# Stage one of a token mixer: rows turned by transposing DMAs instead of TensorE, and a second residual buffer

## The chip, the cores and the metric

The kernel runs on one core of a Trainium2 chip. The metric is the device time of one execution in microseconds (us), the median of several runs. TensorE is called PE in the profile (PEld is its weight load), VectorE DVE, ScalarE ACT, GpSimd POOL, SyncE SP; an engine's name with a q behind it is its sequencer, where DMAs are issued.

## What is computed

The input is a set of 16 images of 256 by 64 complex coefficients. Four steps follow, the last two over 16 x 257 rows of 512 numbers:

```python
h = _L0_tok_ref(x, L0_tok_log_dt, L0_tok_B_ri, L0_tok_inv_A_real, L0_tok_A_imag, 512)
h = jnp.concatenate([jnp.broadcast_to(cls_tok, (h.shape[0], 1, h.shape[2])), h], axis=1)
h = h + _L0_attn_ref(_layernorm(h, axis=-1), L0_attn_gamma, ..., L0_attn_b_skip)
h = h + _L0_ffn_ref(_layernorm(h, axis=-1), L0_ffn_gate_w, ..., L0_ffn_sw_down)
```

`_L0_tok_ref` makes 256 tokens per image out of powers of complex numbers. `_L0_attn_ref` is a gated recurrence along the tokens (`h = (1 - a) * h + a * b`, times a tanh), with an output projection and a skip projection of the normalized row. `_L0_ffn_ref` is a mixture of eight experts of which each row uses two, plus one shared expert that all rows use: `silu(x @ sw_gate) * (x @ sw_up) @ sw_down`.

## The kernel before

Every number that enters a product is split into two fp16 halves, high and low, and a product is three matmuls (high x high, high x low, low x high); `split3` writes them.

There are two stages. **Stage one** walks through the tokens in blocks of 16 tokens of all 16 images, that is 256 rows or two tiles of 128; block 0 is the class token and has one tile. Per block it makes the tokens, runs the recurrence and the shared expert, stores the sum in `out`, chooses two experts per row, and scatters the normalized rows to `x_slots`, sorted by expert. **Stage two** takes 71 tiles of such rows through their experts and adds the results to `out`. The change lies wholly in stage one.

Each engine has its own instruction list, written by hand, and semaphores are all that ties the lists together. A list is a row of bodies, `body(-1)` to `body(17)`; bodies 3 to 13 are a loop of the hardware, the others are written out. A body works on four blocks at once. `body(k)` does, on PE and in this order:

- gate and up products of the shared expert for block k-1 (line 1025 on; six groups m = 0 to 5, PSUM banks 1, 2, 0 in turn), and after group 3 five small products that rank the rows;
- `project(0)` for block k, tile 0: skip and output projection into banks 4 and 5;
- `shared_down(0)` and `shared_down(1)` for block k-1, both into bank 3 (`BD`);
- `project(1)` for block k;
- the turning of the normalized rows of block k+1: 16 transposes through PE (`transposes`, line 982, `x2w` in the trace), which ACT copies to SBUF as `x2T` (line 1238);
- `features` for block k+2: 64 small fp32 products that make the tokens;
- the turning of the second normalized rows of block k, tile 0 (`rows3`, 8 transposes of `x3w`), which ACT copies as `x3T` (line 1244);
- the input products of block k+1 (`win`, 36 matmuls of 256 columns);
- `rows3` for tile 1, and then the router's products of block k (24 matmuls of 8 columns, `gw`), which wait for ACT's copies.

DVE's list for body k: `gprod` and `glow` multiply gate by up and split the result; `choose` and `place` work on the ranks; `stats2` takes mean and variance of block k+1; `tok_p` and `tok_e` are large elementwise products that feed `features` (`tok_p(n, 5)` is what `features(n)` waits for); line 1554 writes the low half of `x2r`. For each tile it then adds the down product to the residual and writes it to `r_o` (line 1560), adds the projections to the residual `h2` (lines 1569, 1570), takes its mean and variance (1572 to 1577), and, when POOL has made the inverse root (lines 927, 928) and ACT the normalized row and its high half (`rows_hi`, lines 1173, 1177), writes the low half (`rows_lo`, line 1450). The recurrence (`scan`) ends the body.

The second `shared_down` waits until DVE has read bank 3 (`c_dev`), because there is one bank; and line 1569 for block k waits until `r_o` has been made from `h2` of block k-1, because there is one `h2`.

SP issues the plain DMAs: the tokens of a block (`hx`), an expert's weights in and their halves out, the rows of `out`. In `body(16)` it also issues eight rounds of two DMAs that write zero rows behind each expert's rows in `x_slots` (lines 824 to 829); each round first loads two addresses from SBUF into registers. Stage two starts when SP has loaded the first tiles (line 799), which wait for DVE's table (`d_tb`).

## Time and profile before

| | |
|---|---|
| median of 3 runs | 1255.03 us (1254.31 to 1255.35) |
| the profiled execution, its own time | 1255.78 us |
| its span in the trace | 1254.1 us |
| PE busy | 1095.0 us, 87% of the span |
| DVE busy | 817.1 us, 65% |
| stage one, first `features` to first expert product | about 75 to 825 us |
| one body of stage one (bodies 4 to 13) | 42.1 us |

The trace is of one execution. A row of a timeline gives start, length, engine, line of the kernel, instruction, and in square brackets how long the engine had been idle before it and what it waited for. Matmuls are pipelined, so two rows of PE overlap a little, and the distance of two starts is the better measure. The granted clock of PE is 1.00 of its full speed from 300 to 700 us; it lies lower in the first 150 us and again between 790 and 800 us.

### The profile page before, as it was taken

What the parts mean: (1) busy time and instruction counts of PE and PEld (TensorE: products, weight loads), DVE (VectorE), ACT (ScalarE), POOL (GpSimd) and SP (SyncE); (2) the same over time, 40 slices, a digit from 0 to 9 for tenths busy, and PEclk for the clock granted to TensorE, in tenths of its full rate; (3) what the DMA queues carried; (4) which work ended last, traced back from release to release, by engine and by line L of the source; (5) the groups of instructions that cost most, each with busy time, mean ns of one, the idle gap of its engine ahead of it and who ended that gap; (6) DMA issues with size and microseconds to landing.
All of it is one profiled execution on the core that took longest, in us unless ns stands there. A gap on an engine that the chain in (4) does not pass through costs nothing.

```text
span 1254.1 us, 27654 instructions
## 1 busy us (share of the span) xinstructions
PE 1095.0 (87%) x8397; PEld 729.3 (58%) x8398; DVE 817.1 (65%) x2123; ACT 408.2 (33%) x724; POOL 412.3 (33%) x352
## 2 busy tenths in 40 slices
PE   3037889999999999999999999759999999999995
PEld 3035566667666766676667656525555555555552
DVE  7955887888788878887888655433444444444442
ACT  4313444435443544355345542301111111111110
POOL 1001221332233123212321221114555555655554
PEclk8556999999999999999999999899999999999998
DMA  7310243233323332333233329847998787878785
GB/s 250 99 32 22 70 139 107 84 130 129 121 76 138 128 111 87 138 120 109 97 138 121 105 104 374 289 113 181 220 222 135 125 134 130 132 126 137 128 129 71
DMA packets 241446, 166.16 MB, mean 132 GB/s; under 512 B 191522, under 2 KB 210338, under 8 KB 239348
## 3 DMA queue, kind: packets, MB, share of 16 engines
q1 hardware_dynamic: 224852, 120.14, 36.3%
q0 software_dynamic: 15504, 36.46, 14.3%
q10 hardware_dynamic: 1040, 8.91, 1.8%
q8 instruction: 28, 0.46, 0.1%
q14 instruction: 22, 0.18, 0.0%
HBM read 53.40 MB, written 79.73 MB: 106 GB/s over the span
## 4 chain that ended last, share of the span: by engine, by line
PE 64%; DVE 11%; ACT 7%; issue 4%; POOL 4%; DMA 2%; SPq 2%; POOLq 0%; DVEq 0%; ACTq 0%
PE bank L974 24%; PE bank L1136 11%; PE bank L1126 10%; PE bank L1127 10%; PE bank L1058 4%; ACT wexp L1244 2%; POOL inv L927 2%; PE bank L996 2%; DVE r_o L1560 2%; DVE h L1569 2%; ACT wexp L1173 2%; DVE h L1570 1%; DVE stat L1572 1%; POOL off L928 1%; DVE wexp L1328 1%
## 5 line engine op out<-in xcount | busy, mean ns | idle before, releaser
L974 PE MATMUL bank<-wexp 128*128 128x256 f16 (+2 forms) x3252 | 410.7, 288 | 12.4 <-DVE yT L1513 4.1
L974 PEld LDWEIGHTS bank<-wexp 128*128 128x128 f16 x3252 | 312.1, 100 | 92.2 <-issue 11.6
L1126 PE MATMUL bank<-wexp,rows_in 128*128 x852 | 256.8, 314 | 9.5 <-DMA rows_in<-x_slots 3.4
L1127 PE MATMUL bank<-wexp,rows_in 128*128 x852 | 256.2, 314 | 0.0
L952 POOL DMA_INDIRECT out<-x2w,rows_in x71 | 113.6, 1600 | 124.8 <-DMA out<-x2w,rows_in 74.8
L940 POOL TENSOR_TENSOR ex<-base,ld 128x8 f32<-128x8 f32 x71 | 120.1, 1691 | 75.4 <-DVE ld L1617 74.7
L1638 DVE SCALAR_TENSOR_TENSOR mixed<-bank,mixed 128x352 f32<-128x352 f32 x71 | 37.3, 525 | 164.0 <-ACT mixed L1285 123.2
L1285 ACT ACTIVATE mixed<-bank 128x352 f32<-128x352 f32 x71 | 32.9, 464 | 302.5 <-PE bank L1127 294.1
L1058 PE MATMUL bank<-wexp 128*128 128x512 f16 x495 | 114.1, 383 | 17.0 <-DVE r_o L1560 17.0
L904 POOL TENSOR_TENSOR inv<-var,power 128x4 f32<-128x4 f32 x17 | 19.1, 1122 | 316.5 <-DVE var L1506 316.5
L1126 PEld LDWEIGHTS bank<-wexp,rows_in 128*128 128x128 f16 x852 | 83.4, 98 | 68.3 <-issue 27.7
L918 POOL DMA_INDIRECT x_slots<-x3w,sl x66 | 91.9, 1392 | 69.5 <-DVE sl L1395 40.0
L1136 PE MATMUL bank<-wexp,gates 128*128 (+1 forms) x477 | 111.7, 379 | 2.6 <-DVE x2w L1633 2.6
L996 PE MATMUL bank<-wexp 64*128 64x64 f32 x1024 | 67.2, 292 | 49.8 <-DVE wexp L1333 49.8
L1127 PEld LDWEIGHTS bank<-wexp,rows_in 128*128 128x128 f16 x852 | 83.5, 98 | 44.3 <-issue 0.3
L927 POOL TENSOR_TENSOR inv<-var,power 128x1 f32<-128x1 f32 x33 | 35.5, 1076 | 183.5 <-DVE var L1577 183.5
L996 PEld LDWEIGHTS bank<-wexp 64*128 64x128 f32 x1024 | 65.0, 205 | 51.9 <-issue 47.1
L1188 ACT ACTIVATE sgs<-bank 128x256 f32<-128x256 f32 (+1 forms) x102 | 38.4, 376 | 164.2 <-PE bank L974 164.2
L1058 PEld LDWEIGHTS bank<-wexp 128*128 128x128 f16 x495 | 46.1, 98 | 77.3 <-DVE r_o L1560 21.7
L1173 ACT ACTIVATE wexp<-h,off,inv 128x512 f32<-128x512 f32 x33 | 26.8, 813 | 168.4 <-POOL off L928 168.4
L1328 DVE TENSOR_TENSOR wexp<-wexp 128x1024 f32 (+1 forms) x64 | 77.8, 1222 | 0.9
L1136 PEld LDWEIGHTS bank<-wexp,gates 128*128 128x128 f16 (+1 forms) x477 | 46.6, 98 | 52.5 <-issue 3.5
(287 smaller groups left out, 1426.2 us busy)
## 6 DMA issues: line engine op xcount, KB each, us to landing
w_halves<-rows_in SPq DMA_DIRECT2D x16, 704.0 KB
wexp<-w_halves ACTq DMA_DIRECT2D x1, 8704.0 KB
wexp<-w_halves SPq DMA_DIRECT2D x8, 1088.0 KB
h_tok<-tokens SPq DMA_DIRECT2D x16, 512.0 KB, 2.7
mixed<-h_tok SPq DMA_DIRECT2D x32, 256.0 KB
out<-r_o SPq DMA_DIRECT2D x32, 256.0 KB
w_halves<-rows_in SPq DMA_DIRECT2D x16, 384.0 KB
x_slots<-zrow SPq DMA_DIRECT2D x8, 768.0 KB, 5.0
```

Of the source, the lines that this page charges most:

```text
L918: nc.gpsimd.indirect_dma_start(out=xs_d.bitcast(I32), out_offset=bass.IndirectOffsetOnAxis(ap=sl[:, i, c:c + 1], axis=0), in_=x3w[:, i, :] ...
L927: link(TT(inv3[:, i:i + 1], var3[:, i:i + 1], power[:, 0, 0:1], ALU.pow))
L940: nc.gpsimd.tensor_tensor(ex[:, b % 2, 0, :], base[:], ld[:, b % 2, :], ALU.pow).then_inc(d_ex, 1)
L952: nc.gpsimd.indirect_dma_start(out=out_rows, out_offset=bass.IndirectOffsetOnAxis(ap=ext[b][:, E:E + 1].bitcast(I32), axis=0), in_=yo[b % ...
L974: last = MM(dst, stat_of(step, a), mov_of(step, b), start=(s_ == 0 and a + b == 0), stop=(s_ == len(steps) - 1 and a == 1))
L996: last = MM(BU[t][:, j * NA:(j + 1) * NA], pp[q, f, j].rearrange("p b c -> p (b c)"), ea[q, f, j, :], start=(f == 0), stop=(f == 1))
L1058: MM(BD[:], gT[:, m, a, t], wsd[:, m, b, :], start=(m == 0 and a + b == 0), stop=False)
L1126: MM(GB[:, 0:H], xT[b][:, a, c, :], wexp[:, u, o:o + H], start=s_, stop=e_)
L1127: last = MM(UB[:, 0:H], xT[b][:, a, c, :], wexp[:, u, o + H:o + 2 * H], start=s_, stop=e_)
L1136: last = MM(DB[:], gT2[b % 4][0:HK[c], a, c, :], wexp[0:HK[c], bass.ds(unit, 2), o:o + D // 2], start=(c == 0 and a + w == 0), stop=(c == ...
L1173: A(xf[:, i, :], h2[:, i, :], ACT.Identity, bias=off3[:, i:i + 1], scale=inv3[:, i:i + 1]).then_inc(c_xf3, 2 // nt)
L1328: ch.do(TT((pp, pt)[f % 2][:, f // 2], cc, hh, ALU.mult))
```

## The change

Four things are changed.

1. PE turns no rows in stage one. SP issues transposing DMAs from `x2r` to `x2T` and from `x3w` to `x3T` (one per tile, four per body), after the other DMAs of its body and before the stores to `out`. Those of `x2T` for block k+1 wait for `project(1)` of block k. PE and ACT lose the transposes and the copies.
2. `h2` has two buffers, used by turns, and `r_o` is gone: the down product is added in place (`down_out`) and `out` is stored from `h2`. The down products have two banks, 3 and 0.
3. The order on PE becomes gate and up, `project(0)`, `shared_down(0)`, `project(1)`, `shared_down(1)`, `features`, `win`, router.
4. On ACT and DVE the work is in another order: block k+1 is normalized in the middle of block k-1's gate and up work, DVE's line for the low half of `x2r` stands there too, `project_out(1)` stands ahead of the last two `tok_p`, and the token copies (`tok_out`) come later on ACT. The loop of the hardware holds two bodies and runs five times (bodies 4 to 13).

The instructions' order, first PE, from the second projection of a body that is written out to its end (body 2 of before, body 3 of the change; both have the same rows there as the bodies of the loop). The names are the program's: `wexp` is the large buffer in which all weights and turned rows of stage one lie, 128x64 x32 are the products of `features`, 128x256 x36 those of `win`. Before:

```order
L1045 MATMUL bank<-wexp,yT 128x512
L1046 MATMUL bank<-wexp,yT 128x512
L1047 MATMUL bank<-wexp,yT 128x512
L1048 MATMUL bank<-brow,ones_row 128x512
L982 MATMUL bank<-ident,x2w 128x128 x16
L996 MATMUL bank<-wexp 128x64 x32
L982 MATMUL bank<-ident,x3w 128x128 x8
L974 MATMUL bank<-wexp 128x256 x36
L982 MATMUL bank<-ident,x3w 128x128 x8
L974 MATMUL bank<-gw,wexp 128x8 x24
```

Of the change, the rows of the same stretch (here with `shared_down(1)`, which follows the second projection):

```order
L1056 MATMUL bank<-wexp,yT 128x512
L1057 MATMUL bank<-wexp,yT 128x512
L1058 MATMUL bank<-wexp,yT 128x512
L1059 MATMUL bank<-brow,ones_row 128x512
L1069 MATMUL bank<-wexp 128x512 x15
L1072 MATMUL bank<-wexp 128x512
L1073 MATMUL bank<-wexp 128x512
L1008 MATMUL bank<-wexp 128x64 x32
L994 MATMUL bank<-wexp 128x256 x36
L994 MATMUL bank<-gw,wexp 128x8 x24
```

The three rows of transposes (`ident`) are gone, and the second down product stands between the second projection and `features`.

Next SP at the end of `body(16)`: the eighth round of zero rows and what follows it. Before:

```order
L826 ISA
L826 REGISTER_ALU
L826 DMA x_slots<-pads 384x16
L828 ISA
L828 DMA x_slots<-zrow 128x3x512
L846 DMA out<-r_o 8x16x512 [waits c_dev]
L846 DMA out<-r_o 8x16x512
L794 DMA w_halves<-rows_in 128x2816 [waits c_wl]
L795 DMA w_halves<-rows_in 128x1536
```

Of the change:

```order
L826 ISA
L826 REGISTER_ALU
L826 DMA x_slots<-pads 384x16
L828 ISA
L828 DMA x_slots<-zrow 128x3x512
L856 DMA_TRANSPOSE wexp<-x3w 128x8x128 [waits c_up,c_rt,c_lo3]
L856 DMA_TRANSPOSE wexp<-x3w 128x8x128 [waits c_lo3]
L866 DMA out<-h 8x16x512 [waits c_dev]
L866 DMA out<-h 8x16x512
```

The two transposing DMAs of `x3w` for block 16 stand behind the last of the eight rounds, where before PE turned these rows.

Last DVE, from the variance of tile 0 on, in the same two bodies. Before (L1577 is that variance and, further down, that of tile 1; L1333 are `tok_p` 4 and 5, L1450 is `rows_lo(0)`, L1560 `r_o`, L1308 `tok_e`):

```order
L1577 TENSOR_SCALAR var<-mv 128x1
L1333 TENSOR_TENSOR wexp<-wexp 128x1024 x2
L1450 SCALAR_TENSOR_TENSOR x3w<-wexp,x3w 128x512
L1560 SCALAR_TENSOR_TENSOR r_o<-bank,h 128x512
L1569 SCALAR_TENSOR_TENSOR h<-bank,ir,mixed 128x512
L1570 SCALAR_TENSOR_TENSOR h<-bank,h 128x512
L1572 BN_STATS stat<-h 128x6
L1574 BN_AGGR mv<-stat 128x2
L1576 TENSOR_SCALAR neg<-mv 128x1
L1577 TENSOR_SCALAR var<-mv 128x1
L1308 TENSOR_TENSOR wexp<-wexp 128x512 x4
```

Of the change (L1514 is the variance, L1326 `tok_p(3)`, L1519 `down_out(0)`, L1443 `rows_lo(0)` and at the end `rows_lo(1)`, L1506 to L1514 `project_out(1)`, L1331 `tok_p` 4 and 5):

```order
L1514 TENSOR_SCALAR var<-mv 128x1
L1326 TENSOR_TENSOR wexp<-wexp 128x1024
L1519 SCALAR_TENSOR_TENSOR h<-bank,h 128x512
L1443 SCALAR_TENSOR_TENSOR x3w<-wexp,x3w 128x512
L1506 SCALAR_TENSOR_TENSOR h<-bank,ir,mixed 128x512
L1507 SCALAR_TENSOR_TENSOR h<-bank,h 128x512
L1509 BN_STATS stat<-h 128x6
L1511 BN_AGGR mv<-stat 128x2
L1513 TENSOR_SCALAR neg<-mv 128x1
L1514 TENSOR_SCALAR var<-mv 128x1
L1331 TENSOR_TENSOR wexp<-wexp 128x1024 x2
L1443 SCALAR_TENSOR_TENSOR x3w<-wexp,x3w 128x512
```

`tok_p` 4 and 5, for which `features` waits, have moved from ahead of `rows_lo(0)` to behind it and behind the whole of `project_out(1)`.

The diff, cut to its core:

```diff
--- before.py
+++ after.py
...
-        LOOP0, LOOP1 = 3, NCH - 2
+        LOOP0, TRIPS = 4, (NCH - 6) // 2
...
+            with eng.Fori(0, TRIPS) as kk:
                 if chain is not None:
-                    chain.enter(k, LOOP0, per)
-                body(k)
+                    chain.enter(kk, 0, per)
...
+                    if has(k + 1):
+                        n = k + 1
+                        sp.wait_ge(c_lo2, n + 1)
+                        apart(sp, c_sps)
+                        at_least(sp, c_out, n * 2)
+                        apart(sp, c_sps)
+                        for i in range(tiles(n)):
+                            sp.dma_start_transpose(x2T[:, i].rearrange("p h k t -> p (h k) t"),
+                                                   x2r[:, i].rearrange("p h d -> p (h d)")).then_inc(c_e2[i], 16)
+                    if has(k):
+                        n = k
+                        at_least(sp, c_up, n * 6)
+                        apart(sp, c_sps)
+                        at_least(sp, c_rt, n)
+                        apart(sp, c_sps)
+                        for i in range(tiles(n)):
+                            sp.wait_ge(c_lo3, n * 2 + (i + 1) * 2 // tiles(n))
+                            apart(sp, c_sps)
+                            sp.dma_start_transpose(x3T[:, i].rearrange("p h k t -> p (h k) t"),
+                                                   x3w[:, i, 0:2 * D]).then_inc(c_e3[i], 16)
...
-                                sp.dma_start(dst, r_o[:, i, :]).then_inc(c_ro, 16)
+                                sp.dma_start(dst, h2[:, 1 - q, i, :]).then_inc(c_ro, 16)
...
-                def rows3(n, i):
-                    done = n * 2 + (2 if tiles(n) == 1 else i + 1)
-                    pe.wait_ge(c_hi3, done)
-                    pe.wait_ge(c_lo3, done)
-                    if i == 1 and has(n - 1):
-                        pe.wait_ge(c_dev, n * 2)
-                    if has(n + 1):
-                        pe.wait_ge(c_e2, (n + 2) * 2)
-                    transposes(BX[i], x3r[:, i]).then_inc(c_t3, 2 // tiles(n))
...
+                        if m == 2:
+                            at_least(pe, c_dev, n * 2)
...
+                    if has(k - 1):
+                        for m in range(SHM + 1):
+                            gate_up_shared(m)
+                            if m == 3:
+                                ranks()
                     if has(k):
                         project(0)
                     if has(k - 1):
                         shared_down(0)
+                    if has(k) and tiles(k) == 2:
+                        project(1)
                     if has(k - 1) and tiles(k - 1) == 2:
                         shared_down(1)
-                    if has(k) and tiles(k) == 2:
-                        project(1)
-                    if has(k + 1):
-                        n = k + 1
-                        pe.wait_ge(c_hi2, n + 1)
-                        pe.wait_ge(c_lo2, n + 1)
-                        at_least(pe, c_e3, n * 2 - 2)
-                        at_least(pe, c_th, n)
-                        for q in range(tiles(n)):
-                            if q == 1 and has(k - 1):
-                                pe.wait_ge(c_sl, k)
-                            transposes((psum[0], BG)[q], x2r[:, q]).then_inc(c_t2, 2 // tiles(n))
...
+                    if has(k + 1):
+                        n, w, nt = k + 1, cols(k + 1), tiles(k + 1)
+                        for i in range(nt):
+                            pe.wait_ge(c_e2[i], turned_rows(n, i))
+                        at_least(pe, c_th, n)
+                        if has(k - 1):
+                            pe.wait_ge(c_sl, k)
+                        for m in range(3):
                             dst = (BG[:, 0:w], BB[:, 0:w], BG[:, TOK:TOK + w])[m]
-                            last = split3(dst, lambda s_, a: win[:, s_, a, m * S:(m + 1) * S],
-                                          lambda s_, b: x2T[:, b, s_, 0:w], range(KD))
-                            if m == 2:
-                                last.then_inc(c_gt, 1)
-                    if has(k) and tiles(k) == 2:
-                        rows3(k, 1)
+                            last = split3(dst.rearrange("p (i t) -> p i t", t=P), lambda s_, a: win[:, s_, a, m * S:(m + 1) * S],
+                                          lambda s_, b: x2T[:, 0:nt, b, s_, :], range(KD))
+                        last.then_inc(c_gt, 1)
                     if has(k):
                         n = k
                         for i in range(tiles(n)):
-                            pe.wait_ge(c_e3, n * 2 + (i + 1) * 2 // tiles(n))
-                            t = slice(i * P, (i + 1) * P)
-                            last = split3(BS[:, i * E:(i + 1) * E], lambda s_, a: x3T[:, a, s_, t],
+                            pe.wait_ge(c_e3[i], turned_rows(n, i))
+                            if tiles(n) == 1:
+                                pe.wait_ge(c_oev, 2)
+                            elif i == 0:
+                                pe.wait_ge(c_oev, n * 2 + 2)
...
+                def normalized(n):
+                    nt = tiles(n)
+                    act.wait_ge(c_pw2, n + 1)
+                    at_least(act, c_lo3, n * 2 - 2)
+                    for i in range(nt):
+                        last = A(xf[:, i, :], hx[:, i, :], ACT.Identity, bias=off2[:, i:i + 1], scale=inv2[:, 0, i:i + 1])
+                    last.then_inc(c_xf2, 1)
+                    act.wait_ge(c_xf2, n + 1)
+                    for i in range(2):
+                        at_least(act, c_e2[i], turned_rows(n - 1, i))
+                    A(x2r[:, 0:nt, 0, :], xf[:, 0:nt, :], ACT.Copy, scale=SX).then_inc(c_hi2, 1)
...
+                        ghigh(n, 2)
+                    if has(k + 1):
+                        normalized(k + 1)
...
+                    if has(k + 1):
+                        n, nt = k + 1, tiles(k + 1)
+                        at_least(act, c_oev, n * 2)
+                        A(hc[:, 0:nt, :], hx[:, 0:nt, :], ACT.Copy).then_inc(c_prom, 1)
...
+                    def down_out(i):
+                        n, nt = k - 1, tiles(k - 1)
+                        v.wait_ge(c_dn, n * 2 + (i + 1) * 2 // nt)
+                        STT(h2[:, 1 - q, i, :], BD[i][:], 1.0 / SW, h2[:, 1 - q, i, :], ALU.mult, ALU.add).then_inc(c_dev, 2 // nt)
...
-                    if has(k - 1):
+                        glow(k - 1, 0)
+                        gprod(k - 1, 2)
+                    elif tokens2:
+                        for f in range(2):
+                            tok_p(k + 2, f)
+                    if isinstance(k, int) and k == -1:
+                        for f in range(5):
+                            tok_e(1, f)
+                    if has(k + 1):
+                        stats2(k + 1)
...
+                    if shared and tokens2:
+                        tok_p(k + 2, 0)
+                    if shared:
+                        glow(k - 1, 1)
+                        gprod(k - 1, 3)
+                        place(k - 1)
+                        if tokens2:
+                            tok_p(k + 2, 1)
+                    if shared:
+                        glow(k - 1, 2)
+                        gprod(k - 1, 4)
+                    if has(k + 1):
+                        n, nt = k + 1, tiles(k + 1)
+                        v.wait_ge(c_hi2, n + 1)
+                        STT(x2r[:, 0:nt, 1, :], xf[:, 0:nt, :], SX, x2r[:, 0:nt, 0, :], ALU.mult, ALU.subtract).then_inc(c_lo2, 1)
...
+                    if tokens2:
+                        tok_p(k + 2, 2)
+                    if has(k):
+                        project_out(0)
+                    if tokens2:
+                        tok_p(k + 2, 3)
+                    if shared:
+                        down_out(0)
+                    if has(k):
+                        rows_lo(k, 0)
+                    if has(k) and tiles(k) == 2:
+                        project_out(1)
+                    if isinstance(k, int) and k == LAST:
+                        table(1)
+                    if tokens2:
+                        tok_p(k + 2, 4)
+                        tok_p(k + 2, 5)
+                    if has(k) and tiles(k) == 2:
+                        rows_lo(k, 1)
+                    if shared and tiles(k - 1) == 2:
+                        down_out(1)
                     if htok(k + 3):
-                        tok_e(k + 3, 4)
+                        for f in range(4):
...
```

## Rows read from the trace of the kernel before

**Rows 1.** The page, part 1: engine, busy time, share, instructions.

```profile
PE 1095.0 (87%) x8397; PEld 729.3 (58%) x8398; DVE 817.1 (65%) x2123; ACT 408.2 (33%) x724; POOL 412.3 (33%) x352
```

**Rows 2.** Timeline of PE, body 6: start, length (us), engine, line, instruction.

```profile
336.91 10.65 PE L974 MATMUL bank<-wexp 128*128 128x256 f16 x96 [0.26 <-issue]
...
359.93 3.41 PE L1058 MATMUL bank<-wexp 128*128 128x512 f16 x15 [0.88 <-DVE r_o L1560]
...
367.48 1.07 PE L982 MATMUL bank<-ident,x2w 128*128 128x128 f16 x16
368.47 3.79 PE L996 MATMUL bank<-wexp 64*128 64x64 f32 x64
...
372.65 4.09 PE L974 MATMUL bank<-wexp 128*128 128x256 f16 x36
...
378.31 0.46 PE L974 MATMUL bank<-gw,wexp 128*128 128x8 f16 x12 [0.83 <-ACT wexp L1244]
379.03 1.16 PE L974 MATMUL bank<-wexp 128*128 128x256 f16 x9 [0.27 <-issue]
```

**Rows 3.** Timeline of DVE, the same body.

```profile
342.78 0.42 DVE L1356 SCALAR_TENSOR_TENSOR gf<-bank,sgs 128x256 f32<-128x256 f32 x1 [1.28 <-ACT sgs L1188]
...
359.19 0.69 DVE L1560 SCALAR_TENSOR_TENSOR r_o<-bank,h 128x512 f32<-128x512 f32 x1 [1.12 <-PE bank L1062]
360.02 0.75 DVE L1569 SCALAR_TENSOR_TENSOR h<-bank,ir,mixed 128x512 f32<-128x512 f32 x1
...
362.72 2.35 DVE L1333 TENSOR_TENSOR wexp<-wexp 128x1024 f32<-128x1024 f32 x2
366.81 0.69 DVE L1450 SCALAR_TENSOR_TENSOR x3w<-wexp,x3w 128x512 f16<-128x512 f32 x1 [1.75 <-ACT x3w L1177]
```

**Rows 4.** Timeline of POOL, the same body.

```profile
349.16 1.03 POOL L904 TENSOR_TENSOR inv<-var,power 128x4 f32<-128x4 f32 x1 [18.25 <-DVE var L1506]
...
362.99 1.38 POOL L927 TENSOR_TENSOR inv<-var,power 128x1 f32<-128x1 f32 x1 [4.09 <-DVE var L1577]
```

**Rows 5.** Timeline of ACT, body 6.

```profile
353.97 1.52 ACT L1226 ACTIVATE wexp<-mixed,off,inv 128x512 f32<-128x512 f32 x2
355.52 1.06 ACT L1230 ACTIVATE x2w<-wexp 128x1024 f16<-128x1024 f32 x1
```

**Rows 6.** Timeline of PE, bodies -1 to 1.

```profile
83.80 1.01 PE L982 MATMUL bank<-ident,x2w 128*128 128x128 f16 x8 [3.46 <-DVE x2w L1554]
...
110.11 7.09 PE L996 MATMUL bank<-wexp 64*128 64x64 f32 x64 [3.12 <-DVE wexp L1333]
...
123.86 4.18 PE L974 MATMUL bank<-wexp 128*128 128x128 f16 x72
...
161.24 3.98 PE L974 MATMUL bank<-wexp 128*128 128x256 f16 x35
```

**Rows 7.** Timeline of PE, the last bodies of stage one.

```profile
725.60 0.17 PE L1032 MATMUL bank<-m,tri 128*128 128x8 f16 x1
...
765.28 0.17 PE L1032 MATMUL bank<-m,tri 128*128 128x8 f16 x1
...
794.90 13.42 PE L974 MATMUL bank<-wexp 128*128 128x256 f16 x96
...
825.17 0.47 PE L1126 MATMUL bank<-wexp,rows_in 128*128 x1 [3.39 <-DMA rows_in<-x_slots]
```

**Rows 8.** Timeline of DVE, body 16.

```profile
772.63 0.27 DVE L1546 CAST runi<-run 128x8 int32<-128x8 f32 x1
```

**Rows 9.** Timeline of SP's issues, body 16.

```profile
774.69 0.72 SPq L826 DMA_DIRECT2D x_slots<-pads  x1
...
805.37 1.98 SPq L846 DMA_DIRECT2D out<-r_o  x2
```

**Rows 10.** Landing times of line 799's transposing DMAs, stage two.

```profile
L799 SPq DMA_TRANSPOSE rows_in<-x_slots x71: 1246/1253/1777, 821.1 to 1215.1; - x71
...
DMA to landing us min/median/max: 3.0/3.1/6.5
```

More of the change, by code:

```diff
@@ L170, in vit_tower @@
         late = Region(high.ap[:, high.at:])
-        x2T = high.take([P, 2, KD, TOK], F16)
-        x3T = high.take([P, 2, KD, TOK], F16)
+        x2T = high.take([P, 2, 2, KD, P], F16)
+        x3T = high.take([P, 2, 2, KD, P], F16)
         gT = high.take([P, SHM + 1, 2, TOK], F16)
@@ L707, in iterate @@
         def iterate(eng, body, chain=None, per=None):
-            body(-1)
+            body(-1, 1)
             for k in range(LOOP0):
-                body(k)
-            with eng.Fori(LOOP0, LOOP1) as k:
+                body(k, k % 2)
+            with eng.Fori(0, TRIPS) as kk:
                 if chain is not None:
-                    chain.enter(k, LOOP0, per)
-                body(k)
+                    chain.enter(kk, 0, per)
+                for r in range(2):
+                    body(kk * 2 + LOOP0 + r, (LOOP0 + r) % 2)
             if chain is not None:
-                chain.leave(LOOP1 - LOOP0)
-            for k in range(LOOP1, LAST + 1):
-                body(k)
+                chain.leave(TRIPS)
+            for k in range(LOOP0 + 2 * TRIPS, LAST + 1):
+                body(k, k % 2)
+        turned_rows = lambda n, i: n * 16 + (16 if i == 0 else 0)
         has = lambda k: not isinstance(k, int) or 0 <= k <= NCH
@@ L976, in split3 @@
                     return last
-                def transposes(bank, rows):
-                    for h in range(2):
-                        for c in range(KD):
-                            last = nc.tensor.transpose(bank[:].bitcast(F16)[:, (h * KD + c) * P:(h * KD + c + 1) * P],
-                                                       rows[:, h, c * P:(c + 1) * P], ident16[:])
-                    return last
                 def features(k):
@@ L1039, in project @@
                         if i == 0:
+                            for j in range(tiles(n)):
+                                pe.wait_ge(c_e2[j], turned_rows(n, j))
                             pe.wait_ge(c_yh, n + 1)
@@ L1231, in body @@
-                    if has(k):
-                        rows_hi(k, 0)
-                    if has(k + 1):
-                        n, nt = k + 1, tiles(k + 1)
-                        at_least(act, c_out, (k + 1) * 2)
-                        for i in range(nt):
-                            act.wait_ge(c_t2, n * 2 + (i + 1) * 2 // nt)
-                            A(x2T[:, :, :, i * P:(i + 1) * P].rearrange("p h k t -> p (h k) t"),
-                              (psum[0], BG)[i][:].bitcast(F16).rearrange("p (c t) -> p c t", t=P), ACT.Copy).then_inc(c_e2, 2 // nt)
@@ L1240, in rows_t @@
[L1240 to L1245 removed]
+                        n = k - 1
+                        silu(n, 1)
+                        ghigh(n, 0)
+                        silu(n, 2)
@@ L1338, in tok_p @@
                             ch.do(ins)
-                def tokens_p(k, f):
-                    if not isinstance(k, int) or k >= 0:
-                        tok_p(k + 2, f)
                 def glow(n, m):
@@ L1536, in body @@
-                    if has(k - 1):
+                        glow(k - 1, 0)
[3 more added lines that the diff above has]
+                            tok_p(k + 2, f)
+                    if isinstance(k, int) and k == -1:
+                        for f in range(5):
+                            tok_e(1, f)
+                    if has(k + 1):
+                        stats2(k + 1)
+                    if isinstance(k, int) and k == -1:
+                        for f in range(6):
+                            tok_p(1, f)
@@ L1537, in body @@
+                    if shared:
+                        glow(k - 1, 3)
+                        gprod(k - 1, 5)
+                        glow(k - 1, 4)
                         glow(k - 1, 5)
```

232 lines of the change are left out of this document (83 added, 149 removed).

## Prediction

> **What bounds the kernel now.** I read the page's first part, then the PE timeline of one steady body with DVE's, POOL's and ACT's of the same stretch, then the two ends of stage one, where the bodies are unlike. PE is busy 1095.0 us of the span, DVE 817.1 [rows 1], but these are means over two stages and the change is in stage one alone. Body 6 lasts from one gate and up start to the next, 336.91 to 379.03, 42.12 us, and PE is nearly full in it [rows 2]. What it loses is four things: the second down product waits 0.88 for `r_o` (359.93); the 16 transposes hold it from 367.48 to 368.47, 0.99; the two times 8 transposes of `x3w` cost some 0.5 each, half of that; the router waits 0.83 for ACT's copy (378.31) [rows 2]. Together 3.7: without them PE alone would need 38.4 us. DVE has waits too, but small ones: 1.28, 1.12 and 1.75 us are the three that I use [rows 3]. Both engines are close to the bound, so an edit that frees PE is worth only what DVE lets it be worth.
>
> **The steady body.** Removing the transposes, the one-bank wait and the copies frees the 3.7 us of PE. The question is when `features` may start, since it waits for DVE's `tok_p(5)`. Before, `tok_p` 4 and 5 end at 362.72 + 2.35 = 365.07 [rows 3], ahead of the 367.48 at which PE came to its transposes: PE never waited. The order of the change puts behind the variance of tile 0: `tok_p(3)`, `down_out(0)`, `rows_lo(0)`, all of `project_out(1)`, and only then `tok_p` 4 and 5. The chain on DVE begins with `gprod(1)`, which the second gate and up group releases, 342.78 - 336.91 = 5.87 us after the body's start [rows 2, 3]; up to there nothing changes. From there, step by step to the end of `tok_p(5)`:
> - before, the stretch from there to `project_out(0)` is 360.02 - 342.78 = 17.24 [rows 3]
> - three things leave it: the wait for the down product, 1.12, `r_o` itself, 0.83 from its start to the next, and one `tok_p`, half of 2.35 [rows 3]: -3.1
> - block k+1 is normalized in the middle of the gate and up work. ACT's two pieces, 1.52 and 1.06 [rows 5], now stand between the `silu`s that DVE's next products wait for, behind POOL's power (1.03 at 349.16 [rows 4]). Bounds: 0 if DVE's own work covers them all, 2.6 if none. DVE has a `tok_p` and the ranks to do meanwhile, so I take about a quarter: +0.6
> - `project_out(0)` as before, 360.02 to 362.72: +2.7 [rows 3]
> - from its variance to the start of `rows_lo(0)`, POOL's and ACT's chain: 366.81 - 362.72 = 4.09 [rows 3]. Before, 2.35 of `tok_p` filled it and 1.75 was waiting; now one `tok_p` and `down_out(0)` fill 1.2 + 0.7 and 2.2 is waiting: +4.1
> - `rows_lo(0)` by its row, `project_out(1)` as long as that of tile 0, and `tok_p` 4 and 5: 0.7 + 2.7 + 2.35 [rows 3]: +5.7
>
> Sum 17.2 - 3.1 + 0.6 + 2.7 + 4.1 + 5.7 = 27.2, against 365.07 - 342.78 = 22.3 before. `tok_p(5)` ends 5.9 + 27.2 = 33.1 us after the start. From the start of `features` to the end of the body PE took 379.03 - 368.47 = 10.56 with the router's wait of 0.83 and 1.0 of transposes in it, so 8.7 without [rows 2]. Of its 38.4 us it has then done 29.7 when it comes to `features`, and waits 3.4. The body is 33.1 + 8.7 = 41.8 us. So I expect the stall on PE not to go but to move: small losses become one wait of about 3.4 us for DVE ahead of `features`, and **a body shrinks by 0.3 us only**. Bodies 3 to 13: -3.3 us.
>
> **The transposing DMAs in it.** Before has none in stage one; the nearest rows are stage two's, one 128x1024 tile each: 1.25 us of SP per issue, 3.0 to 6.5 to landing, median 3.1 [rows 10]. Those of `x2T` are released by `project(1)`, which ends one down product (3.41 and a little, 359.93 [rows 2]) ahead of the 29.7, at about 26; the second lands at 26 + 1.3 + 3.1 = 30.4, and `win` wants it behind `features`, at 33.1 + 3.8 = 36.9 (3.79 [rows 2]). The variance of tile 1 is made at 33.1 - 2.35 = 30.8, `rows_lo(1)` ends 4.1 + 0.7 later, at 35.5, `x3T` of tile 1 lands at 38.6, and the router wants it at about 40.9. Both are hidden; cover 6.5 and 2.3 us. Behind them on SP stand the stores to `out` and the next tokens, which nobody needs within the body. ACT is freed of its copies, 0: it was not last.
>
> A rule of the Trainium skill speaks against this part: VectorE: DVE Perf Modes, The three transpose paths and Rules for kernel authors, gives 390 ns for a 128x128 turned by TensorE and 1309 ns by DMA, and says to use TensorE where PSUM will do as the destination. By that figure the eight blocks of a tile would take about 10.5 us (an estimate from it), past both covers: `x3T` would come near 46.0 instead of 40.9, and 14 bodies of 5 us more would make the sum some 70 us higher. The trace doesn't agree: eight land in 3.1 us, at most 6.5 [rows 10].
>
> **The edges.** Body -1 and 0: ACT normalizes ahead of the token copies, so that the 3.46 us in which PE waits for `x2w` [rows 6] partly go; `features` in body 0 waits already for DVE (3.12 [rows 6]) and will more. Bounds -3.5 and +1; I take -2. Body 1 (37.4 us, 123.86 to 161.24 [rows 6]) is short because block 0 has one tile; DVE has all of the tokens' work in it, so DVE's later `tok_p(5)` now sets it, near 41: +3.5. Body 2: +1, the same half covered. Body 14: no `tok_e` is left, DVE has room: -1.5. Body 15 (725.60 to 765.28 between the ranks' products, 39.7 us [rows 7]) has no `features` and no `tok_p`, so nothing of DVE takes the place of the freed 3.7: -3.8.
>
> Body 16 is the costly one. SP's eight rounds begin when DVE has cast the counts (772.63 + 0.27 [rows 8]) and end when SP issues the store at 805.37 [rows 9]: 32.4 us, bound by SP itself, first round at 774.69. Before, PE turned block 16's rows and its gate and up products started at 794.90 [rows 7], in the middle of them. Now the two DMAs of `x3T(16)` stand behind the eighth round. Second issue 805.37 + 1.25 = 806.6, landing 3.1 later, 809.8, router 0.5 [rows 10]: gate and up starts at about 810.5, on the clock of before. **+15.6 us.** DVE and ACT have nothing else then; the whole of it is on the path, since stage two's first product (825.17, after 3.39 for its DMA [rows 7]) waits for the table that ends this chain. Body 17: 0.
>
> Sum: -2 + 3.5 + 1 - 3.3 - 1.5 - 3.8 + 15.6 = +9.5. The profiled execution took 1255.78 by its own time with a span of 1254.1 (the table), so the sum holds against either, and against the median 1255.0 it gives **1264.5 us**.
>
> **The rivals.** (A) Faster: PE stays the bound. The 2.2 of waiting and the 0.6 are estimates; if DVE does without both, `tok_p(5)` ends near 30.3, and the body is 39.0, close to PE's 38.4. Then 11 x (-3.1) = -34 and the edges' +12.8: 1234 us. It is on the other side as soon as a body is under 40.96 us (-1.16 x 11 = -12.8). For it: the chain of 4.09 has 1.38 for POOL's power with DVE busy beside it [rows 4], against 1.03 for one four times as wide. Against it: `project_out(1)`'s 2.7 is no wait, and moves whatever the waits do. Chance of the faster side 0.2; at half of the two waits it is 40.4 and 1249.
>
> (B) Slower still: POOL's power for `stats2` is held up by `tok_p(0)`, which now stands right behind the variance. 349.16 took 1.03, 362.99 took 1.38 beside `tok_p` on DVE [rows 4]; if it has to let one whole `tok_p` by (1.18), normalizing is that much later, and with half of it covered the body is 42.3: +0.5 x 14 = +7, 1271.5 us. SBUF — State Buffer, Who interferes with whom, of the Trainium skill says so: a DVE operation with two inputs from SBUF and a GpSimd operation that reads SBUF block each other fully; the 1.38 agrees and does not prove it. Chance 0.12.
>
> (C) The DMAs are not hidden: with the slowest landing, 6.5 [rows 10], `x3T` comes at 42.0 instead of 40.9: +1.1 per body, 14 bodies, 1280 us. Chance 0.04. (The figure that the Trainium skill gives above is this case in a larger size.) (D) The rounds on SP come out shorter, because fewer other DMAs are under way: at 6 us less it is 1258.5, which lies in my case's own range.
>
> **How the numbers follow.** My case 0.6, by itself 1257 to 1271: 0.4 us more or less per body is 4.4, the edges' bounds are some 3, and D takes up to 6. A 0.2, B 0.12, C 0.04, a near cancellation of A and the edge 0.04. The time is that of my case. The range leaves out C and the lower half of A: 1247 to 1276. Within 0.2% (2.5 us, about what can be told from no change) lie the cancellation, the low tail of my case and the high one of A: 0.12. Faster 0.2, slower 0.68.
>
> **What would show it.** PE: no `ident` rows in stage one, one wait of 3 to 4 us for DVE's `tok_p` (L1331) ahead of each `features`, none at the second down product; bodies 41.8 apart. DVE: `rows_lo(0)` idle 2 us before it, for ACT. SP: the transposing DMAs landing in about 3 us, SP waiting ahead of them. Body 16: PE idle for some 20 us, then released by a DMA. I am wrong if the wait ahead of `features` is under 2 us, if gate and up waits for a DMA in the steady bodies, or if body 16 is not some 55 us long.

## The result, and the profile after

The changed kernel takes 1320.4 us (median of 4 runs, 1317.3 to 1324.2) against 1254.7 us: ratio 1.0525, 95% interval 1.0505 to 1.0544. It is 66 us slower; 9.5 had been forecast, and the range ended at 1276. The profiled execution has a span of 1318.0 us.

The timeline of PE in the changed kernel, body 7, the rows that answer to [rows 2] (L994 was L974, L1008 `features` was L996):

```profile
355.66 10.65 PE L994 MATMUL bank<-wexp 128*128 128x256 f16 x96 [0.23 <-issue]
...
378.38 2.76 PE L994 MATMUL bank<-wexp 128*128 128x512 f16 x12 [0.57 <-DVE h L1507]
...
389.05 5.67 PE L1008 MATMUL bank<-wexp 64*128 64x64 f32 x64 [3.07 <-DVE wexp L1331]
394.65 5.47 PE L994 MATMUL bank<-wexp 128*128 128x256 f16 x36
...
399.95 0.75 PE L994 MATMUL bank<-gw,wexp 128*128 128x8 f16 x24
400.56 10.64 PE L994 MATMUL bank<-wexp 128*128 128x256 f16 x96
```

The transposes and their waits are gone, and one wait of 3.07 us stands ahead of `features`, for DVE's `tok_p(5)`. But `features` takes 5.67 us and `win` 5.47, where [rows 2] has 3.79 and 4.09 for the same 64 and 36 matmuls. This body is 400.56 - 355.66 = 44.9 us long; the mean of the eleven steady ones is 45.9 (504.7 / 11, table below).

DVE in the same body, which answers to [rows 3] (L1443 is `rows_lo`, L1331 `tok_p` 4 and 5):

```profile
383.25 0.69 DVE L1443 SCALAR_TENSOR_TENSOR x3w<-wexp,x3w 128x512 f16<-128x512 f32 x1 [1.67 <-ACT x3w L1185]
...
386.56 2.35 DVE L1331 TENSOR_TENSOR wexp<-wexp 128x1024 f32<-128x1024 f32 x2
```

`tok_p(5)` ends at 386.56 + 2.35 = 388.91, 33.25 us after the body's start. 33.1 had been worked out.

The view by windows of the body before this one (body 6), whose `features` starts at 342.12 after an idle 3.04 us. Behind the length stand the busy times of PE, PEld, DVE, ACT and POOL; the third number from the end is the granted clock of PE:

```profile
342.00:344.00 2.00, 1.88 (x24) 1.88 (x25) 0.35 (x1) 1.90 (x3) 0.04 (x1) 0.72 0.00 0
344.00:346.00 2.00, 2.00 (x22) 2.00 (x22) 2.00 (x4) 1.32 (x3) 0.00 (x0) 0.50 0.19 40
346.00:348.00 2.00, 2.00 (x24) 2.00 (x22) 1.88 (x4) 0.00 (x0) 0.00 (x0) 0.50 0.72 104
...
350.00:352.00 2.00, 2.00 (x11) 1.45 (x10) 1.53 (x5) 0.00 (x0) 0.00 (x0) 0.50 0.81 306
352.00:354.00 2.00, 2.00 (x15) 1.59 (x14) 0.00 (x0) 0.00 (x0) 0.00 (x0) 0.72 0.27 109
354.00:356.00 2.00, 1.77 (x36) 1.57 (x35) 0.17 (x1) 0.84 (x2) 0.00 (x0) 1.00 0.55 126
```

From 344 to 352 PE is busy without a gap, but the granted clock is 0.50, the lower of its two levels (1.2 of 2.4 GHz), and 64 and 36 matmuls take 6.46 and 6.32 us in this body; at 354 it is back at 1.00. Before the change it was 1.00 throughout the stretch of [rows 2].

SP, then PE, at the end of body 16 (answering to [rows 7, 9]; L826 and L828 are the rounds of zero rows, L856 the transposing DMAs of `x3w`):

```profile
824.59 8.05 SPq L826 DMA_DIRECT2D x_slots<-pads  x1
...
853.93 0.40 SPq L828 DMA_DIRECT2D x_slots<-zrow  x1
854.61 3.67 SPq L856 DMA_TRANSPOSE wexp<-x3w  x2
```

```profile
858.99 0.48 PE L994 MATMUL bank<-gw,wexp 128*128 128x8 f16 x12 [27.82 <-DMA wexp<-x3w]
860.21 0.48 PE L994 MATMUL bank<-gw,wexp 128*128 128x8 f16 x12 [0.74 <-DMA wexp<-x3w]
860.55 12.85 PE L994 MATMUL bank<-wexp 128*128 128x256 f16 x96
873.23 0.17 PE L1040 MATMUL bank<-m,tri 128*128 128x8 f16 x1
...
890.30 0.47 PE L1133 MATMUL bank<-wexp,rows_in 128*128 x1 [3.44 <-DMA rows_in<-x_slots]
```

PE stands for 27.82 us until the DMAs behind the eighth round land. Stage two's first product comes at 890.30 instead of 825.17: the whole loss of 65.1 us lies ahead of it (the two spans differ by 63.9). By the distances between the ranks' products (L1032 before, L1040 after) it is made up so:

| stretch | forecast | measured |
|---|---|---|
| up to body 1's ranks (130.52, now 127.21) | -2 | -3.3 |
| to body 2's and body 3's | +3.5, +1 | +6.6, +3.1 |
| eleven steady bodies (ranks of body 3 to those of 14) | -3.3 | +41.8 (463.0 to 504.7) |
| to 15's, 16's | -1.5, -3.8 | +2.7, -4.2 |
| to 17's (holds the wait in body 16) | +15.6 | +18.4 |
| from there to stage two | 0 | 0.0 |

### The profile page after: what moved, and what is told of

It is laid out like the page before. It is cut to its first block, busy times and chain, and to the rows that moved or that the text cites. A ratio compares the mean times of both kernels' runs of the same rounds, so it can differ in the third digit from the quotient of the medians.

```text
span 1318.0 us, 26490 instructions
## 1 busy us (share of the span) xinstructions
PE 1118.8 (85%) x7869; PEld 743.6 (56%) x7870; DVE 814.4 (62%) x2123; ACT 346.2 (26%) x658; POOL 402.7 (31%) x352
## 3 DMA queue, kind: packets, MB, share of 16 engines
q1 hardware_dynamic: 294548, 137.45, 41.8%
## 4 chain that ended last, share of the span: by engine, by line
PE 57%; DVE 18%; issue 6%; ACT 4%; SPq 4%; POOL 4%; DMA 1%; POOLq 0%; DVEq 0%; ACTq 0%
PE bank L994 20%; PE bank L1143 10%; PE bank L1133 9%; PE bank L1134 9%; PE bank L1008 8%; DVE wexp L1331 3%; POOL inv L924 2%; DVE wexp L1326 2%; DVE h L1506 2%; DVE h L1507 2%; DVE stat L1487 1%; ACT wexp L1209 1%; DVE stat L1509 1%; POOL inv L947 1%; DVE x2w L1558 1%
## 5 line engine op out<-in xcount | busy, mean ns | idle before, releaser
L994 PE MATMUL bank<-wexp 128*128 128x256 f16 (+2 forms) x3252 | 434.7, 298 | 17.3 <-DVE h L1507 11.0
L994 PEld LDWEIGHTS bank<-wexp 128*128 128x128 f16 x3252 | 322.8, 103 | 110.7 <-DVE h L1507 15.0
L1008 PE MATMUL bank<-wexp 64*128 64x64 f32 x1024 | 102.9, 390 | 102.2 <-DVE wexp L1331 102.2
L1008 PEld LDWEIGHTS bank<-wexp 64*128 64x128 f32 x1024 | 100.0, 300 | 107.0 <-issue 79.9
L924 POOL TENSOR_TENSOR inv<-var,power 128x4 f32<-128x4 f32 x17 | 29.2, 1716 | 389.2 <-DVE var L1499 389.2
L938 POOL DMA_INDIRECT x_slots<-x3w,sl x66 | 75.9, 1149 | 92.3 <-DVE sl L1388 75.1
L947 POOL TENSOR_TENSOR inv<-var,power 128x1 f32<-128x1 f32 x33 | 41.8, 1267 | 162.5 <-DVE var L1514 162.5
L1349 DVE SCALAR_TENSOR_TENSOR gf<-bank,sgs 128x256 f32<-128x256 f32 (+1 forms) x102 | 42.5, 416 | 73.7 <-ACT sgs L1196 68.5
L1069 PEld LDWEIGHTS bank<-wexp 128*128 128x128 f16 x495 | 45.7, 98 | 61.7 <-issue 7.0
L1326 DVE TENSOR_TENSOR wexp<-wexp 128x1024 f32 (+1 forms) x64 | 77.8, 1220 | 0.8 <-issue 0.2
```

The costliest lines, as they stand in the source:

```text
L924: link(TT(inv2[:], var2[:], power[:], ALU.pow))
L938: nc.gpsimd.indirect_dma_start(out=xs_d.bitcast(I32), out_offset=bass.IndirectOffsetOnAxis(ap=sl[:, i, c:c + 1], axis=0), in_=x3w[:, i, :] ...
L947: link(TT(inv3[:, i:i + 1], var3[:, i:i + 1], power[:, 0, 0:1], ALU.pow))
L994: last = MM(dst, stat_of(step, a), mov_of(step, b), start=(s_ == 0 and a + b == 0), stop=(s_ == len(steps) - 1 and a == 1))
L1008: last = MM(BU[t][:, j * NA:(j + 1) * NA], pp[q, f, j].rearrange("p b c -> p (b c)"), ea[q, f, j, :], start=(f == 0), stop=(f == 1))
L1069: MM(BD[i][:], gT[:, m, a, t], wsd[:, m, b, :], start=(m == 0 and a + b == 0), stop=False)
```

## The experiments

Two theories stood: **clock** (PE's new wait lowers its clock, which makes the work behind the wait slow) and **traffic** (the transposing DMAs, new here, slow PE's own reads). Edits are to the changed kernel where nothing else is said; all ratios are to the kernel before.

### warm: the wait filled with matmuls

```diff
+                        for r in range(12):
+                            MM(BU[r % 2][:], gT[:, 0, 0, 0:P], wsd[:, 0, 0, :], start=True, stop=True)
                     pe.wait_ge(c_tokp, n)
```

> The changed kernel with twelve more matmuls of 128x512 on PE ahead of each features from body 1 on, in the time in which PE waits for DVE; their sums are overwritten. Theory clock: features and win take 5.4 to 7.1 and 5.3 to 6.3 us instead of 3.8 and 4.1 because PE stood idle for 3.0 us ahead of them and the granted clock fell to 0.50; with PE busy there they take 3.8 and 4.1 again, the body is 33.25 + 8.7 = 42 us instead of 45.9, and the kernel takes about 1320 - 11 x 3.9 - 3 x 3 = 1268 us. Theory traffic: the transposing DMAs, new in this stretch, slow PE's reads; features and win stay as they are, and so does the time, 1320 us.

1269.2 us, ratio 1.0112 (1.0094 to 1.0130): 51 us less than the changed kernel for more work on PE. Timeline of PE, body 7 (L1004 are the filling matmuls, L1010 `features`):

```profile
367.23 2.76 PE L1004 MATMUL bank<-wexp 128*128 128x512 f16 x12
370.28 3.79 PE L1010 MATMUL bank<-wexp 64*128 64x64 f32 x64 [0.29 <-DVE wexp L1333]
374.00 4.11 PE L994 MATMUL bank<-wexp 128*128 128x256 f16 x36
```

`features` and `win` are back at 3.79 and 4.11 us beside the same DMAs, and the mean of ten bodies is 41.7 us, where 41.8 had been forecast for the change itself. Stage two's first product comes at 834.28, 9.1 us later than before the change, where the forecast had 9.5; parts of that lie off in either direction (eleven steady bodies -5.1, body 16 +16.9), so a total so close is in part luck. `features` at its old time beside the same DMAs speaks for clock and against traffic.

### before_late: the kernel before, with the late tok_p

```diff
-                        if htok(k + 2) and i == 0:
+                        if htok(k + 2) and i == 1:
                             tokens_p(k, 4)
                             tokens_p(k, 5)
```

> The kernel before with one change: tok_p 4 and 5 stand behind the second variance on DVE, as in the changed kernel. PE still turns all rows in stage one, there are no transposing DMAs in it. tok_p(5) comes some 5 us later, at about 33.5 us of the body, and features waits 2 us or more. Theory clock: features and win then run partly at the half clock as in the changed kernel, 5.5 to 6.5 us each; body 46 to 48 us, 1300 to 1320 us. Theory traffic: features stays at 3.8 and win at 4.1 us, only the wait is added: body 44 to 44.5 us, about 1280 us.

1384.5 us, ratio 1.1030 (1.1012 to 1.1049). Timeline of PE in one body:

```profile
364.31 1.07 PE L982 MATMUL bank<-ident,x2w 128*128 128x128 f16 x16
369.61 7.09 PE L996 MATMUL bank<-wexp 64*128 64x64 f32 x64 [4.22 <-DVE wexp L1333]
376.63 1.04 PE L982 MATMUL bank<-ident,x3w 128*128 128x128 f16 x8
377.46 5.20 PE L974 MATMUL bank<-wexp 128*128 128x256 f16 x36
```

No transposing DMA is in this stage, and `features` takes 7.09 us behind a wait of 4.22. Traffic has fallen as the cause. The time missed my range by 64 us: I had counted on 2 us of waiting or more and on the slowing of the changed kernel, and both are larger here (bodies of 51.2 us).

### late_warm: that wait filled too

```diff
+                        for r in range(18):
+                            MM(BU[r % 2][:], gT[:, 0, 0, 0:P], wsd[:, 0, 0, :], start=True, stop=True)
                     pe.wait_ge(c_tokp, n)
```

> before_late with eighteen more matmuls of 128x512 on PE ahead of features from body 1 on, in its wait of 4.2 us; their sums are overwritten. It parts the two costs of a late tok_p(5) in a kernel without transposing DMAs: the wait, which stays, and the clock, which should not fall. Theory clock: features 3.8 us instead of 7.1, win 4.1 instead of 5.2, the eight transposes 0.6 instead of 1.0: body 51.2 - 4.8 = 46.4 us, 1384 - 13 x 4.8 = 1322 us. If something else in the late order made PE slow: less than 1 us per body.

1318.1 us, ratio 1.0475 (1.0445 to 1.0506); bodies 46.4 us, as worked out:

```profile
347.31 4.05 PE L992 MATMUL bank<-wexp 128*128 128x512 f16 x18
351.63 3.79 PE L998 MATMUL bank<-wexp 64*128 64x64 f32 x64 [0.27 <-DVE wexp L1335]
...
355.81 4.09 PE L974 MATMUL bank<-wexp 128*128 128x256 f16 x36
```

So of the 9.1 us that the late `tok_p` costs a body of the kernel before, 4.8 are the clock and 4.3 the wait. The same late `tok_p` is paid for twice.

### tokp_back: only the two tok_p moved back

```diff
                         down_out(0)
+                    if tokens2:
+                        tok_p(k + 2, 4)
+                        tok_p(k + 2, 5)
                     if has(k):
                         rows_lo(k, 0)
...
-                    if tokens2:
-                        tok_p(k + 2, 4)
-                        tok_p(k + 2, 5)
```

> The changed kernel with tok_p 4 and 5 back in their old place on DVE, behind tile 0's down_out and ahead of rows_lo(0) and project_out(1). Theory clock: features finds its operands ready (about 28 us into the body, PE comes at 29.4), its clock stays full, and features and win take 3.8 and 4.1 us. The next wait is the router's, for the transposing DMA of x3T tile 1, since rows_lo(1) now has no tok_p ahead of it to hide POOL's and ACT's chain: about 2.5 us; body about 40.5 us, or 43 if this wait costs clock as well; time 1255 to 1290 us. Theory traffic: features and win stay near 6 and 5.5 us without a wait ahead of them, body at least 42.5 us, more likely 44.

1244.6 us, ratio 0.9926 (0.9903 to 0.9949): 76 us less than the change, 0.7% below the kernel before, and below the range that I had given (1255 to 1290). Timeline of PE:

```profile
352.48 3.90 PE L1008 MATMUL bank<-wexp 64*128 64x64 f32 x64
356.31 4.11 PE L994 MATMUL bank<-wexp 128*128 128x256 f16 x36
360.25 0.75 PE L994 MATMUL bank<-gw,wexp 128*128 128x8 f16 x24
...
385.58 2.76 PE L994 MATMUL bank<-wexp 128*128 128x512 f16 x12 [1.86 <-DVE h L1507]
```

There is no wait ahead of `features`; the router's wait of 2.5 us that I had expected didn't come, and a wait of 1.86 for DVE's read of banks 4 and 5 did. The mean body is 40.3 us. The eleven steady bodies together are 22 us shorter than before the change; body 16, whose wait this edit leaves, gives 18.5 of them back.

### tokp_turn: the transposes put back on PE, empty

```diff
+                        for r in range(32):
+                            nc.tensor.transpose(BU[r // 8 % 2][:].bitcast(F16)[:, r % 8 * P:(r % 8 + 1) * P],
+                                                gT[:, 0, 0, 0:P], ident16[:])
                     pe.wait_ge(c_tokp, n)
```

> As tokp_back, with 32 transposes of 128x128 on PE ahead of features from body 1 on, whose results are overwritten: as many as the kernel before did in a body, in one run and with nothing to wait for. It tells what PE's time for turning is worth where DVE no longer holds PE up. They cost PE some 1.9 us per body (the kernel before: 0.99 for 16). If the freed PE time is what tokp_back gained: the bodies go from 40.1 to 41 to 42 us, 1256 to 1266 us. If the gain lies in the second bank and the new order, and PE's time had been covered by DVE: less than 0.5 us per body, under 1250 us. In neither case does the clock fall.

1244.6 us, ratio 0.9902 (0.9876 to 0.9927), as tokp_back; mean body 40.5 instead of 40.3 us. Timeline of PE:

```profile
346.79 2.76 PE L994 MATMUL bank<-wexp 128*128 128x512 f16 x12 [0.57 <-DVE h L1510]
...
354.33 1.96 PE L1004 MATMUL bank<-ident,wexp 128*128 128x128 f16 x32
```

The 1.96 us of PE time for 32 transposes, which the change set out to free, cost 0.3 us net per body. The wait for DVE ahead of the second projection takes up most of it: its mean in ten bodies falls from 1.65 to 0.56 us, since PE comes there later. The 0.3 also holds a gain by the clock: behind that wait tokp_back has its twelve matmuls at 4.37 and 4.26 us instead of 2.76 in two of the ten bodies, this kernel in none. Without that, PE's time would cost some 0.6 us per body (an estimate: 3.1 us in ten bodies on top of the 0.3). This kernel doesn't bring back ACT's copies nor the waits for them, so it says nothing on those. What tokp_back gained in the steady bodies (42.1 to 40.3 us) therefore lies for the most part in the rest (second bank, second residual buffer, order, no copies), which no run parted.

### project_first: the read of banks 4 and 5 one tok_p sooner

```diff
-                    if tokens2:
-                        tok_p(k + 2, 2)
                     if has(k):
                         project_out(0)
                     if tokens2:
+                        tok_p(k + 2, 2)
                         tok_p(k + 2, 3)
```

> As tokp_back, with project_out(0) ahead of tok_p(2) on DVE. In tokp_back PE waits 1.9 us in most bodies for DVE's read of banks 4 and 5 (L1507), ahead of the second projection; this read now comes one tok_p, 1.2 us, sooner. If that wait sets the body: -0.8 to -1.2 us in each of 11 bodies, 1231 to 1236 us. If DVE's own sum sets it (some 36 to 37 us busy in a body of 40): less than 4 us in all, since features and the recurrence come no sooner.

1241.1 us, ratio 0.9874 (0.9848 to 0.9900); not clearly below tokp_back. The mean body is 40.2 us: the wait for L1507 fell from 1.9 to 0.6 us, and others took its place: one of 0.6 ahead of the second down product for `down_out` (L1519), 0.2 for the split products (L1342) and 0.3 for the transposing DMA of `x3w`. PE is busy 38.3 us of a body's 40.2, close to the 38.4 that the prediction had as its bound; the waits for DVE add 1.4.

### edge5, best, best_act: body 16

```diff
+                            if e == 4:
+                                turn_x3(k)
```

`turn_x3` holds the lines of the two transposing DMAs of `x3w` and their waits; for block 16 it is called there, in the loop over the eight rounds, and no longer behind it.

> The changed kernel, with the two transposing DMAs of x3T for block 16 issued behind the fifth of SP's eight rounds instead of behind the eighth. The rows are ready at about that time (rows_lo(1) ended 21 us after the rounds began, five rounds take some 24). If the wait behind the rounds is what body 16 costs: gate and up starts three rounds, 10 us, sooner, 1310 us. If the DMAs only wait behind the rounds' own transfers in the queue: less than 4 us.

1313.9 us, ratio 1.0483 (1.0440 to 1.0525), 6.5 us below the change. PE behind its wait, and stage two's first product:

```profile
849.76 0.48 PE L998 MATMUL bank<-gw,wexp 128*128 128x8 f16 x12 [17.97 <-DMA wexp<-x3w]
...
880.32 0.47 PE L1137 MATMUL bank<-wexp,rows_in 128*128 x1 [3.09 <-DMA rows_in<-x_slots]
```

The wait is 17.97 instead of 27.82 us, and stage two starts 10.0 us sooner, as expected. The span is only 7.8 us shorter; where stage two gives 2 us back was not followed.

> project_first and edge5 together. The two lie in different bodies, so the gains should add: the time of project_first less 7 to 10 us, 1222 to 1230 us. If the steady bodies' state shifts the edge: less than 5 us below project_first.

The three edits together (tokp_back, project_first, edge5): 1229.6 us, ratio 0.9808 (0.9770 to 0.9846), 11.5 us below project_first. In the profiles body 16 is 8.3 us shorter; another 3.2 lie in bodies 1 and 2, which are the same code in both, where `features` of body 1 took 5.26 us instead of 7.02 behind the same wait of 2.89. They are no gain of the edit.

```diff
+                    last16 = isinstance(k, int) and k == NCH
+                    if last16:
+                        rows_hi(k, 1, q)
...
-                            if e == 4:
+                            if e == 3:
```

> As best, and in body 16 ACT normalizes tile 1 ahead of the high half of the expert weights, for which it waited 6 us on a DMA, and SP issues x3T(16) behind the fourth round instead of the fifth. The rows are ready some 4 us sooner and the DMAs go out one round sooner: 3.4 us below best. If the rows are still late, because ACT's high half of tile 0 waits for the scatter's DMA: 0 to 1 us.

1227.6 us, ratio 0.9795 (0.9773 to 0.9818). Body 16 shrinks from 51.4 to 48.0 us in the profile, the 3.4 expected; the times of the two can't be told apart. It is 28 us below the kernel before and 93 below the change.

### best_warm: the long waits filled

```diff
+                    if isinstance(k, int) and k == 0:
+                        for r in range(36):
+                            MM(BD[r % 2][:], win[:, 0, 0, 0:P], wskip[:, 0, 0, :], start=True, stop=True)
...
+                        if isinstance(k, int) and k == NCH:
+                            for r in range(44):
+                                MM(BU[r % 2][:], gT[:, 0, 0, 0:P], wsd[:, 0, 0, :], start=True, stop=True)
```

> best_act with matmuls of 128x512 in PE's two long waits outside the steady bodies: 36 in body 0 ahead of features (a wait of 10.5 us), 44 in body 16 ahead of the router (a wait of some 14 us); their sums are overwritten. In best_act the clock is 0.50 behind both. Body 0: features 3.8 instead of 7.1 and win 4.1 instead of 5.1. Body 16: 2.1 us less for gate and up. If both lie on the path: 1227.6 - 6.4 = 1221 us. If DVE sets the first bodies, only body 16 counts: 1225.5 us.

1228.2 us, ratio 0.9772 (0.9745 to 0.9800): no gain that can be told. Timeline of PE, body 0 (L1007 are the filling matmuls, L1015 `features`):

```profile
93.69 7.94 PE L1007 MATMUL bank<-wexp 128*128 128x512 f16 x36
105.54 7.09 PE L1015 MATMUL bank<-wexp 64*128 64x64 f32 x64 [3.90 <-DVE wexp L1344]
```

The run didn't test what it was meant to: the matmuls filled too little of the wait. 3.90 us of it stayed, in body 16 6.30, and behind both the clock was low as before. Whether these edges gain by a full clock stays open.

## Why the prediction was wrong

**The step that failed** is the one in "The steady body" that took the work behind `features`' start, "10.56 with the router's wait of 0.83 and 1.0 of transposes in it, so 8.7 without [rows 2]", at the durations of a PE that doesn't wait. Behind the wait of 3.4 us ahead of it, which the same paragraph forecasts (3.07 measured), the clock falls, and the 8.7 become 400.56 - 389.05 = 11.5 in the body shown and 355.66 - 342.12 = 13.5 in the one before it. Over eleven bodies the steady term was -3.3 and is +41.8. Warm gives the proof by difference: with the wait filled by matmuls and the order kept, PE's clock stays up, the bodies are 41.7 us, as forecast, and 51 us of the 66 are gone.

The evidence lay in the rows that I showed. [rows 6] has `features` at 7.09 us behind a wait of 3.12, beside 3.79 in [rows 2], and [rows 7] has 13.42 for the products that take 10.65 in [rows 2]. I used the first for its wait for DVE and didn't ask why the 64 matmuls took 7.09. The Trainium skill states the rule (TensorE: Matmul & The Clock Gate, Why this matters for your kernels): gaps in which PE stands idle between bursts of matmuls put it back to the half clock. The trace agrees: the granted clock is 0.50 behind the gap of 3.04 us here.

**DVE's chain** was right: `tok_p(5)` at 33.25 us (33.1 forecast), and the stall moved from four small places to one, but for 0.57 us ahead of the second projection. Two terms were off and nearly cancel: the stretch up to `project_out(0)` took 15.3 instead of 14.7 us, the one from its variance to `rows_lo(0)` 3.7 instead of 4.1 (`rows_lo(0)` waits 1.67, 2.2 forecast).

**The transposing DMAs** were hidden in the steady bodies, as forecast. The view of PE's waits, bodies 3 to 14 (in total, times, longest), names none for them:

```profile
PE bank L1008 <- DVE wexp L1331: 36.1, 12, 3.1
PE bank L994 <- DVE h L1507: 5.7, 11, 0.8
PE bank L1120 <- DVE matches L1407: 1.3, 1, 1.3
PE bank L994 <- issue: 0.9, 4, 0.3
```

The median landing of those of `x3w` was 3.0 us, at most 4.3, of those of `x2w` 3.3 and 4.5. Rival C fell. The Trainium skill's figure of 1309 ns for one 128x128 block by DMA (VectorE: DVE Perf Modes, The three transpose paths) is no price per block here: eight blocks in one DMA landed in 3.0 us.

**Bodies 2 and 14** were mis-sized for the same reason (+3.1 and +2.7 for +1 and -1.5): in warm they come to -1.8 and -0.6. **Body 1** has the wait (5.14 us) and the half clock too (`features` 7.09) and came to +6.6 for +3.5, but warm doesn't part the two there: its twelve matmuls left 2.44 us of that wait, `features` took 6.29, and the body was no shorter (+6.4). Body 15, which has no `features`, came as forecast (-4.2 for -3.8).

**Body 16** was right in its mechanism and low by 2.8 us: +18.4 for +15.6. The second round's issue took 8.05 us instead of 5.49 (before, at 777.71) and made up most of it; rival D had the rounds shorter, not longer. PE's wait is 27.82 us where some 20 were forecast, and from gate and up to gate and up (801.50 to 860.55) the body is 59.1 long, not some 55. Edge5 shows that the wait behind the rounds is the cause.

**Rival B** (POOL's power held up by `tok_p(0)`) happened without mattering. POOL, then DVE, in body 7:

```profile
366.67 1.96 POOL L924 TENSOR_TENSOR inv<-var,power 128x4 f32<-128x4 f32 x1 [24.64 <-DVE var L1499]
```

```profile
366.53 1.23 DVE L1326 TENSOR_TENSOR wexp<-wexp 128x1024 f32 x1
```

The power's median went from 1.03 to 1.83 us; here it ends 0.87 us after the `tok_p` that began just ahead of it. If that operation had held it up whole, it would have ended its own 1.03 later; spans on POOL are rough, so this is near a full block. The Trainium skill says that a DVE instruction with two inputs from SBUF contends with a GpSimd instruction that reads SBUF (SBUF — State Buffer, Who interferes with whom), and the trace agrees. DVE's chain came at 33.25 us with it.

**Rival A**, the faster side, did not come by its own condition: `rows_lo(0)` still waited, and `tok_p(5)` ended at 33.25, not near 30.3. What kept the change on the slow side was the order of `tok_p` 4 and 5: tokp_back, with all of the rest of the change, is faster than the kernel before.

## What to carry to other kernels

Where a forecast puts one longer wait of PE in the place of several short ones, price the matmuls behind it at both clock levels, by rows of the same shape behind a wait elsewhere in the trace; idle time in one piece can cost about its own length again (4.3 us of waiting and 4.8 of clock per body in before_late). Look for the DVE operation that feeds PE's next burst before freeing PE of work: here two operations moved by some 5 us decided between 5% slower and 1% faster, and the PE time freed was worth less than 1 us per body. Before a step is moved to another queue, look at what that queue does in the written-out bodies, not only in the loop.

## What was not expected of the hardware

Extra matmuls made a kernel faster by 4% (warm against the change), and by 5% in late_warm against before_late. In tokp_back waits of 1.86 us stood ahead of the second projection in eight bodies: five with no loss behind them (2.76 us for its twelve matmuls, as in the changed kernel behind 0.57), three with 4.26 to 4.45 us; the granted clock was 0.50 from 426 to 428 in the first of these. This view is of those twelve matmuls in one body without the loss and two with it.

```profile
345.25 2.76 PE L994 MATMUL bank<-wexp 128*128 128x512 f16 x12 [1.86 <-DVE h L1507]
...
425.90 4.37 PE L994 MATMUL bank<-wexp 128*128 128x512 f16 x12 [1.86 <-DVE h L1507]
...
506.59 4.26 PE L994 MATMUL bank<-wexp 128*128 128x512 f16 x12 [1.86 <-DVE h L1507]
```

The same wait at the same place cost 1.5 to 1.7 us in three bodies and nothing in five, and nothing here shows why. It is one reason why its bodies differ (39 to 41.6 us) while those of project_first, with shorter waits, alternate between 39.8 and 40.7.
